# Attention and a LoRA feed-forward on one core: scores also in the projections' bank, row sums inverted on turned blocks, one sum over four key tiles, a new order in the unit

## The reference

```python
q = (hidden_states @ Wq).reshape(b, s, 32, 32)
kv = hidden_states @ Wkv;  k, v = kv[..., :32], kv[..., 32:]
scores = einsum('bqhd,bkd->bhqk', q, k) * 32 ** -0.5
scores = where(causal, scores + slopes * (key_pos - query_pos), -inf)
out = einsum('bhqk,bkd->bqhd', softmax(scores), v).reshape(b, s, h) @ Wo
x = layernorm(x + out)
x = layernorm(x + x @ W.T + b + lora_of_the_chosen_rank(x))
```

## Time and profile before

| what | value |
|---|---|
| median of 3 runs | 3776.58 us (3774.8 to 3776.71) |
| the profiled execution | 3775.03 us |
| its span in the trace | 3773.2 us |
| attention, first to last score tile | 68.4 to 2863.5 us |
| TensorE busy by the records | 3582.0 us (95%) |
| VectorE, ScalarE, GpSimd busy | 2415.6, 1927.6, 1358.9 us |
| mean granted TensorE clock | 0.984 |

### The profile page before, as it was taken

The page is one execution under the profiler, slowest core; times in us unless marked ns, Lnnn a source line. Parts: engine busy times, 40 slices in busy tenths (PEclk is TensorE's granted clock), DMA queues, the critical chain, the costliest instruction groups (busy, mean ns, idle before and its releaser), DMA issues. The chain is left out here.

```text
span 3773.2 us, 56666 instructions
## 1 busy us (share of the span) xinstructions
PE 3582.0 (95%) x21057; PEld 2207.2 (58%) x21057; DVE 2415.6 (64%) x5438; ACT 1927.6 (51%) x3252; POOL 1358.9 (36%) x419
## 2 busy tenths in 40 slices
PE   5899999999999999899999999999995999999998
PEld 4555554455444444555554455544432888989987
DVE  4777777777776763777777777777742444444444
ACT  2656656666676756656666666676764101001000
POOL 1114444544455544124445554454552011011010
PEclk8999999999999999999999999999997999999999
DMA  2121110010000011111110000000003121121221
GB/s 85 46 60 32 49 32 24 24 38 23 21 15 21 15 35 32 49 57 32 49 32 24 24 15 23 21 15 21 10 7 123 45 67 55 62 67 50 67 67 40
DMA packets 157358, 148.11 MB, mean 39 GB/s; under 512 B 8356, under 2 KB 140452, under 8 KB 155016
## 3 DMA queue, kind: packets, MB, share of 16 engines
q1 hardware_dynamic: 157128, 145.07, 13.1%
HBM read 94.13 MB, written 33.62 MB: 34 GB/s over the span
## 5 line engine op out<-in xcount | busy, mean ns | idle before, releaser
L507 ACT ACTIVATE prob<-ps_s,alibi 128x512 f32<-128x512 f32 (+3 forms) x2560 | 1525.5, 623 | 868.6 <-PE ps_s L777 435.7
L452 POOL TENSOR_TENSOR prob<-prob 128x2048 f32<-128x2048 f32 (+1 forms) x240 | 1046.8, 4362 | 1091.4 <-ACT prob L507 1091.4
L587 DVE TENSOR_REDUCE mxp<-ps_a 128x1 f32<-128x512 f32 x1536 | 984.1, 682 | 384.4 <-PE ps_a L707 376.1
L774 PE MATMUL ps_s<-qst,kexp 97*128 97x512 f32 (+3 forms) x2560 | 1047.9, 417 | 42.5 <-ACT prob L507 28.4
L707 PE MATMUL ps_a<-kmax,qst 97*128 97x512 f32 (+3 forms) x2560 | 961.9, 396 | 38.8 <-DVE mxp L590 23.1
L774 PEld LDWEIGHTS ps_s<-qst,kexp 97*128 97x128 f32 x2560 | 481.6, 189 | 788.5 <-ACT prob L507 613.5
L719 PE MATMUL ps_o<-prob,val 128*32 128x512 f32 (+3 forms) x5120 | 602.1, 542 | 6.0 <-ACT prob L507 6.0
L590 DVE CUSTOM_DVE_ANT_0 ps_a<-ps_a,maska 128x128 f32<-128x128 f32 (+3 forms) x1024 | 495.4, 503 | 163.0 <-PE ps_a L707 130.1
L707 PEld LDWEIGHTS ps_a<-kmax,qst 97*128 97x128 f32 x2560 | 489.3, 194 | 113.4 <-DVE mxp L590 47.2
L972 POOL TENSOR_TENSOR hb_sb<-h_sb,bias_b 128x1024 f32<-128x1024 f32 x32 | 76.8, 2401 | 792.7 <-DVE z_sb L1116 732.4
L719 PE MATMUL ps_sum<-prob,ones 128*32 128x512 f32 (+3 forms) x3200 | 347.0, 513 | 0.0
(11 more groups left out here) (147 smaller groups left out, 3673.7 us busy)
## 6 DMA issues: line engine op xcount, KB each, us to landing
wq_raw<-in_L_attn_Wq SPq DMA_DIRECT2D x64, 512.0 KB, 3.9
xs<-in_L_attn_hidden_states SPq DMA_DIRECT2D x8, 2048.0 KB, 8.1
qst<-qst SPq DMA_DIRECT2D x64, 256.0 KB
att_scratch<-at_sb SPq DMA_DIRECT2D x64, 256.0 KB, 2.4
at_raw<-att_scratch SPq DMA_DIRECT2D x32, 512.0 KB, 5.2
x_sb<-in_L_attn_hidden_states SPq DMA_DIRECT2D x32, 512.0 KB, 4.2
out<-z_sb SPq DMA_DIRECT2D x32, 512.0 KB, 3.1
z_sb<-in_L_attn_Wo SPq DMA_DIRECT2D x4, 512.0 KB, 5.4
```

The costliest lines, as they stand in the source:

```text
L452: nc.gpsimd.tensor_tensor(even[:, :, c1:], even[:, :, c1:], odd[:, :, c1:], ALU.add).then_inc(pair_done, 1)
L507: nc.scalar.activation(prob[slot_of(steps + k)][:, h, c0:], ps_s[h % 2][:, c0:], ACT.Exp, bias=alibi_of(g, h, k - full_tiles(g))).then_inc ...
L587: nc.vector.tensor_reduce(top, ps, AX.X, ALU.max).then_inc(a_done, 1)
L774: last = nc.tensor.matmul(bank[:, c0:], kexp[0:KR, at:at + P], qst[g % 3][0:KR, h, c0:], start=True, stop=not diagonal)
```

## The change

- Score tiles may use `ps_m` as a third bank, from a slot that `third_from` gives (the last QE or VT, plus THIRD) to the end of the unit; `score_places` takes, for each tile, the bank whose last use is longest ago, and TensorE waits for that use's exponential. The next unit's first projection waits for the last exponential out of `ps_m`.
- In units of 16 key tiles, GpSimd adds two pairs to a quad (ADDQ) and one product sums the four tiles (SQ).
- The row sums are equal on the 32 partitions of a head. VectorE now turns `ps_sum` in 32x32 blocks, takes reciprocals of one column of each block, and turns them back with a broadcast. The copy into `s_sb` is gone.
- `PROBS` is 8, and the tables of slots have other numbers.

```diff
-PROBS = 6
+PROBS = 8
+def adds_until(g, k):
+    pair = k // 2
+    quad = pair // 2
+    if quad < quads_summed(g):
+        return adds_before(g) + 3 * quad + 1 + pair % 2
+    return adds_before(g) + quads_summed(g) + pair + 1
-CHUNKS_AHEAD = (8, 13, 23, 27)
-A_END = (9, 17, 25, 33)
-A_FROM = (11, 18, 26, 34)
-Q_AT = ((0, 0.5), (0, 1), (0, 1.25), (1, 1.5))
-QE_AT = ((3, 1), (7, 2), (9, 3), (11, 5))
-CT_AT = (11, 18, 30, 38)
-X_AT = ((7, 0.5), (9, 1.25), (19, 2), (22, 3))
-KV_AT = (11, 25, 35, 46)
-VT_AT = (17, 27, 40, 47)
-PV_AT = (1, 1, 1, 1)
-SM_AT = (1, 1, 3, 3)
-WS_AT = (5, 17, 27, 33)
-RECIP_AT = ((0, 2, 3, 8, 11), (6, 16, 25, 29, 30), (22, 27, 44, 45, 46), (20, 36, 60, 61, 62))
+CHUNKS_AHEAD = (7, 14, 18, 19)
+A_END = (8, 17, 31, 41)
+A_FROM = (13, 18, 31, 41)
+Q_AT = ((0, 0.5), (0, 1), (1, 1.25), (0, 1.75))
+QE_AT = ((3, 1), (7, 2), (9, 3), (12, 4))
+CT_AT = (12, 22, 35, 42)
+X_AT = ((4, 0.25), (8, 1.75), (19, 1.5), (19, 3.25))
+THIRD = (6, 6, 2, 4)
+QUADS = (0, 0, 0, 1)
+QUAD_AT = 7
+KV_AT = (10, 23, 33, 41)
+VT_AT = (17, 28, 47, 49)
+PV_AT = (1, 1, 2, 1)
+SM_AT = (2, 1, 2, 1)
+WS_AT = (5, 21, 31, 28)
+RECIP_AT = ((0, 2, 3, 4, 11), (0, 2, 3, 5, 14), (0, 2, 5, 7, 18), (0, 2, 4, 5, 20))
+def third_from(g):
+    if g + 2 >= UNITS:
+        return 0
+    s = seg_of(g) % NSEG
+    return (VT_AT[s] if prepares(g) else QE_AT[s][0] + (GH - 1) * QE_AT[s][1]) + THIRD[s]
+def score_places():
+    last = [None, None, None]
+    places = []
+    for g in range(UNITS):
+        if g + 2 < UNITS:
+            last[2] = None
+        for slot in range(GH * ktiles(g)):
+            free = range(3 if slot >= third_from(g) else 2)
+            bank = min(free, key=lambda b: -1 if last[b] is None else last[b])
+            places.append((bank, last[bank]))
+            last[bank] = len(places) - 1
+    return places
...
+            if k >= QUAD_AT and (k - QUAD_AT) % 4 == 0 and (k - QUAD_AT) // 4 < quads and h == SM_AT[s]:
+                out.append(("SQ", (k - QUAD_AT) // 4))
+        if k % 4 == 3 and k // 4 < quads:
+            out.append(("ADDQ", k // 4))
...
                     if what == "OE":
-                        act.wait_ge(sm_done, START + steps + ktiles(g))
+                        act.wait_ge(pv_done, START + steps + ktiles(g))
                         act.wait_ge(at_done, START + g)
                         nc.scalar.activation(o_sb[:], ps_o[:], ACT.Copy).then_inc(o_copied, 1)
-                        nc.scalar.activation(s_sb[:], ps_sum[:], ACT.Copy).then_inc(o_copied, 1)
...
-                nc.vector.reciprocal(r_sb[:, cols], s_sb[:, cols]).then_inc(r_done, 1)
+                if part == 0:
+                    dve.wait_ge(sm_done, START + steps_before(g + 1))
+                    nc.vector.transpose(sum_t[:].rearrange("p b d -> p (b d)"), ps_sum[:]).then_inc(sum_turned, 1)
+                elif part == 1:
+                    dve.wait_ge(sum_turned, START + g + 1)
+                    nc.vector.reciprocal(inv_t[:], sum_t[:, :, 0]).then_inc(inv_done, 1)
+                elif part == 2:
+                    dve.wait_ge(inv_done, START + g + 1)
+                    dve.wait_ge(at_done, START + g)
+                    nc.vector.transpose(r_sb[:].rearrange("p (b d) -> p b d", d=DH),
+                                        inv_t[:].unsqueeze(2).broadcast_to([P, QB // DH, DH])).then_inc(r_done, 1)
...
                     if what == "S":
-                        pe.wait_ge(e_done, START + max(0, GH * (steps + k) + h - 1))
+                        if before is not None:
+                            pe.wait_ge(e_done, START + before + 1)
+                        elif place == 2 and prepares(g):
+                            pe.wait_ge(vt_done, START + seg_of(g) + 2)
+                        elif place == 2:
+                            pe.wait_ge(ql_done, START + GH * min(UNITS, g + 3))
...
                     if what == "PV":
-                        if arg == ktiles(g) - 1:
-                            pe.wait_ge(e_done, START + GH * (steps + arg + 1))
+                        pe.wait_ge(e_done, START + GH * (steps + arg + 1))
```

More of the change, by code:

```diff
@@ L72, in pairs_summed, with quads_summed, adds_in, adds_before @@
     return ktiles(g) // 2 - 1 if full_tiles(g) else 0
-def pairs_before(g):
-    return sum(pairs_summed(x) for x in range(g))
+def quads_summed(g):
+    return QUADS[seg_of(g) % NSEG]
+def adds_in(g):
+    return pairs_summed(g) + quads_summed(g)
+def adds_before(g):
+    return sum(adds_in(x) for x in range(g))
+def adds_until(g, k):
[4 more added lines that the diff above has]
+    return adds_before(g) + quads_summed(g) + pair + 1
 def ring(sg):
@@ L166, in plan_unit @@
     recip_at = {x: part for part, x in enumerate(RECIP_AT[s])}
-    summed = pairs_summed(g)
+    summed, quads = pairs_summed(g), quads_summed(g)
     for k in range(n):
@@ L265, in attention @@
         ps_m = pb(ctx, "ps_m", [P, QB])
+        ps_s.append(ps_m)
+        places = score_places()
         counters = []
@@ L300, in attention @@
         o_copied = counter("o_copied")
+        sum_turned = counter("sum_turned")
+        inv_done = counter("inv_done")
         r_done = counter("r_done")
@@ L429, in divide @@
             def divide(g):
-                pool.wait_ge(r_done, START + QT * (g + 1))
+                pool.wait_ge(r_done, START + g + 1)
+                pool.wait_ge(o_copied, START + g + 1)
                 pool.wait_ge(at_out, START + 16 * g)
@@ L453, in step @@
                                                 ALU.add).then_inc(pair_done, 1)
+                    if what == "ADDQ":
+                        one, two = (prob[slot_of(steps + 4 * arg + i)] for i in (0, 2))
+                        pool.wait_ge(pair_done, START + adds_until(g, 4 * arg + 3))
+                        nc.gpsimd.tensor_tensor(one[:], one[:], two[:], ALU.add).then_inc(pair_done, 1)
             units(prologue, step, lambda count: divide(UNITS - 1))
@@ L739, in prologue, with in_third @@
                 turn_max(0, FIRST - 1)
+            def in_third(g):
+                return max([i + 1 for i in range(tiles_before(g)) if places[i][0] == 2], default=0)
             def step(g, plan, count):
@@ L753, in step @@
                     if what == "Q":
+                        if arg == 0 and in_third(g):
+                            pe.wait_ge(e_done, START + in_third(g))
                         if arg == 0 and prepares(g - 1):
@@ L767, in step @@
                         c0 = max(0, k - full_tiles(g)) * P
-                        bank = ps_s[h % 2]
+                        place, before = places[GH * (steps + k) + h]
+                        bank = ps_s[place]
                         if arg == (0, 0):
                             pe.wait_ge(c_in, START + 16 * (g + 1))
-                        pe.wait_ge(e_done, START + max(0, GH * (steps + k) + h - 1))
+                        if before is not None:
[4 more added lines that the diff above has]
+                            pe.wait_ge(ql_done, START + GH * min(UNITS, g + 3))
                         diagonal = k >= full_tiles(g)
@@ L779, in step @@
                     if what == "PV":
-                        if arg == ktiles(g) - 1:
-                            pe.wait_ge(e_done, START + GH * (steps + arg + 1))
+                        pe.wait_ge(e_done, START + GH * (steps + arg + 1))
                         if arg == 0:
-                            pe.wait_ge(o_copied, START + 2 * g)
+                            pe.wait_ge(o_copied, START + g)
                         over_keys(g, ps_o, val[:, key_tile(g, arg)], arg).then_inc(pv_done, 1)
+                    if what in ("SM", "SP", "SQ") and arg == 0:
+                        pe.wait_ge(sum_turned, START + g)
                     if what == "SM":
+                        pe.wait_ge(e_done, START + GH * (steps + arg + 1))
                         over_keys(g, ps_sum, ones[:], arg).then_inc(sm_done, 1)
                     if what == "SP":
-                        pe.wait_ge(pair_done, START + pairs_before(g) + arg + 1)
+                        pe.wait_ge(pair_done, START + adds_until(g, 2 * arg + 1))
                         over_keys(g, ps_sum, ones[:], 2 * arg).then_inc(sm_done, 2)
+                    if what == "SQ":
+                        pe.wait_ge(pair_done, START + adds_until(g, 4 * arg + 3) + 1)
+                        over_keys(g, ps_sum, ones[:], 4 * arg).then_inc(sm_done, 4)
             units(prologue, step, lambda count: None)
```

10 lines of the change are left out of this document (4 added, 6 removed).

## The result

| kernel | median, us | lowest to highest | ratio to before, 95% interval |
|---|---|---|---|
| before | 3776.64 | 3774.8 to 3778.94 | |
| changed | 3690.52 | 3688.47 to 3707.25 | 0.9783 [0.9768, 0.9797] |

A forecast was written before the change was run, and what follows sets the result against it. TensorE's own order of work was taken as the frame, with 231 us of waits inside it. Terms 48 + 13 + 14 + 9 + 14.5 + 3 = 101.5 us off 3776.6 gave 3675; range for 8 in 10: 3615 to 3725.

The forecast's parts named there:

- third bank: Scores also in `ps_m` late in units: ScalarE has three tiles queued across a product, fewer TensorE waits, 48 us.
- quad: Units of 16: GpSimd adds replace one row-sum product of 1.19 us on TensorE; 13 us, bounds 3 and 19.
- inversion, units of 4 key tiles: Row sums inverted on turned blocks shorten VectorE's chain in units of 4 key tiles: 16 x 0.9 = 14 us.
- VT later than KV: Unit 29: eight slots between KV and VT remove a 6.2 us wait and the lower clock behind it; 9 us.
- other units at ends of segments: Units 13, 15, 21, 23 and twins lose waits at VT or reciprocals on VectorE; 14.5 us, bounds 0 and 25.
- end of attention: From the last reciprocal to the division's end, a ScalarE copy and 3.39 us become shorter; 3 us, bounds 0 and 3.4.
- met before: TensorE's added waits for exponentials ahead of products: already met by the preceding score tile's wait, except with three banks; costed at nothing.
- Rival 3: Units of 16: GpSimd late with the four-tile sum, products wait, 48 us go; 3723 us, chance 0.09.
- taking 0.94 out of that chain brings the whole unit forward by it: Units of 4 key tiles: VectorE's last reciprocal in slot 8 goes, so each unit ends 0.9 us earlier.
- rival 1: Whole order fits better: waits ahead of the bank's opening halve, all behind it go; 155 us, 3621, chance 0.13.
- Rival 2: Waits move to ScalarE, whose exponentials become the pace; only 51 us faster, 3725, chance 0.11.
- Rival 4: More short waits between matmul groups lower the clock in 48 units, 4.3 us each; slower, 3880, chance 0.05.

The follow-up runs named there:

- the second experiment: Changed kernel with SM_AT back from 2 to 1 and CT_AT from 12 to 11 in units of 4 key tiles: 3690.49 us, ratio 0.9771.
- The first experiment: Changed kernel with row-sum products moved away from the products with the values (SM_AT 3) in units of 12 and 16: 3718.77 us, ratio 0.9846.

## Why the prediction was nearly right

| term | forecast, us | measured, us |
|---|---|---|
| third bank | 48 | 37 alone; 111 in the new order |
| quad | 13 | 13.7 (13.0 in the units of 16) |
| inversion, units of 4 key tiles | 14 | plain units 0.2 longer; alone 0.1 shorter, 5 in the whole kernel |
| VT later than KV | 9 | alone: unit 29 8.5, whole kernel 7.2 |
| other units at ends of segments | 14.5 | 1.4 longer (13, 15, 21, 23 and twins) |
| end of attention | 3 | 2.8 |
| row sums joined to the other product | 0 | 28 |

**Third bank.** The step from waits to gain held in kind, with less in size. Alone the bank took 0.5 off a plain unit of 8, 0.4 off one of 12 and 1.3 off one of 16 (32.9, 48.8 and 62.5 us), where the sum had 0.45, 0.8 and 1.7. In units of 12 slot 20 begins 0.57 us late, since the bank's first tile waits for the last copy of q, for which the prediction had taken off 0.3. Units 62 and 63 gained 3.5 and 1.7 alone, not 4 each; the latter has 6.8 us at half the clock. What failed is that the bank was costed on the order of before: the new order asks more of it, and without it would have lost 25 us. The added waits ahead of the products, which the prediction put at nothing as "met before", are often not met (387 weight loads wait), but cost TensorE nothing that shows.

**Quad.** The size is right, partly by luck. The prediction took one lone product of 1.19 away and lost a third of it to waits. The product that went was one of a joined pair, worth 2.04 - 1.19 = 0.85, and a plain unit gained more than that, 1.05, since slot 33 is 0.2 shorter as well (2.23 for 2.43). Units 62 and 63 gave 0.1 and -2.1. The quad's own product is in time in plain units; the later one of slot 41 is not quite, at no cost. Rival 3 came true in unit 63, where no chunks stand between the score tiles.

**Inversion.** The durations were right. The step that failed is "taking 0.94 out of that chain brings the whole unit forward by it". VectorE's chain did get shorter, but the next wait stood 0.3 us behind: a score tile that waits for its bank. In the alone version this is shown. In the changed kernel more is against it. The last chunks are reached 0.3 to 0.6 us later, with the two of one slot together. With the old row sums and CT, in the second experiment's timeline, TensorE waits there:

```profile
144.11 0.51 PE L774 MATMUL ps_a<-kmax,qst 97*128 97x512 f32 x1 [0.70 <-DVE mxp L647]
```

Slot 5 takes 3.62 us there, 2.60 before. That the order of the chunks is what takes the gain was only argued. The third bank with the old table of chunks and the turned inversion would test it; it was not tried. The other units of 4 (5 to 7 and 37 to 39) are 7.4 us shorter in the changed kernel, but not all by the inversion: 7 and 39 lose 2.3 and 2.5 with it alone, while 5 and 37 (1.3 each) lose a wait of 1.39 us at VT, which the new places of X, KV and VT take away. And alone, in the new slots of R, the inversion costs 0.3 us in each plain unit of 8 and 12, which the sum did not have.

**VT.** Right in place, size and clock: of the six waits of the earlier trace rows only the one of 3.2 us ahead of unit 0 is left, and the clock in unit 29 is 1.00. Attention has six stretches at a clock of 0.5 before (37.5 us together) and seven after (30.7 us); the one of 13.7 us behind the wait of the earlier trace rows and those of units 5 and 37 are gone, those in units 17, 45, 48 and 63 are new.

**Other units.** Mis-sized by 16 us. Fewer reciprocals on VectorE bought nothing there: 21 and 53 got 1.1 longer each. In unit 13 the wait at VT was only 0.50 us; slot 26 begins 0.8 us earlier, but the unit ends only 0.2 earlier; half of what is lost is in its last slot, 1.94 us (1.66). All units of 8 have that: the new table puts a chunk into the last slot, which is why plain ones take 33.2 and not 32.9. Unit 45 got 1.4 longer by the clock: it has a stretch of 3.4 us at 0.5 from slot 28, which 13 has not. Units 15 and 47 differ by 4 us in both kernels in the same way (10.2 us at 0.5 in 15 alone). The first experiment takes 64.1 and 62.5 in 21 and 53, so joining is not what made them longer; what did was not settled.

**End of attention**, in the timeline after, against the earlier trace rows:

```profile
2784.15 0.72 DVE L669 STREAM_TRANSPOSE sum_t<-ps_sum 128x512 f32<-128x512 f32 x1 [50.59 <-PE ps_sum L786]
2784.90 0.25 DVE L672 RECIPROCAL inv_t<-sum_t 128x16 f32<-128x16 f32 x1
2785.19 0.71 DVE L676 STREAM_TRANSPOSE r_sb<-inv_t 128x512 f32<-128x512 f32 x1
2785.98 1.26 POOL L487 TENSOR_TENSOR at_sb<-o_sb,r_sb 128x512 f32<-128x512 f32 x1 [4.47 <-DVE r_sb L676]
```

From the first operation of the inversion to the division's end it is 3.09 us, and ScalarE's copy lies beside it. From the end of the last row-sum product to the division's end it is 3.15 us, against 5.91 before: 2.8 us won.

**What was not in the sum.** `PV_AT` and `SM_AT` were read as numbers of slots and costed at nothing, though they put two products side by side. This is the largest omission, 28 us of gain. It offset what the inversion and the other units did not bring, so that the total is nearer than its terms is luck. Two numbers beside the sum are off: the 70 us of waits that bound the bank's term add up to 64 by the counts given, and the 3200 and 3072 records are the row-sum products of all units, not of those of 16.

**The rivals.** Plain units of 12 and 16 did better than forecast, as rival 1 has it, but by joined products rather than by its mechanism: ahead of slot 28 unit 27 gained 1.4 us (slot 28 begins 27.7 us into the unit, 29.1 before), and without the quad, which took the row sums out of slots 19 and 27, nothing (29.3). Rival 2 appears in the second line of the waits but did not cancel the gain. Rival 4 did not decide the changed kernel: its plain units in the windows above show a clock of 1.00 with three banks in rotation, against the Trainium skill's case ("TensorE: Matmul & The Clock Gate", A second HAM failure mode). Of the other plain units one, 17, has a stretch at 0.5 (49.0 us for 47.3). But the rival's mechanism is real here: the old order with bank and joined products has 24 stretches, ten of them behind a wait of 1.4 to 1.6 us for the third bank in units of 12. Its price was too high, 4.3 us a drop from unit 29, where a stretch of 3.4 us costs 1.4.

## What to carry to other kernels

A buffer and the order that uses it have to be costed together. Five of the kernels read: 3777 (old order), 3741 (with the bank), 3797 (bank and joined products), 3801 (new order without the bank), 3691 (new order with it).

Where one engine's chain ends a unit, find the wait that stands next behind it before counting the relief: 0.76 us won on VectorE came out as 0.1, since a score bank was 0.3 us away.

A table of slots is also a table of neighbours. When two entries fall on the same slot, cost the pair from a row that shows it, and ask how long the other engines are left without work.

## What the runs showed of the hardware

Two products over 128x512, each in four groups of 32 columns, cost 2.04 us of TensorE side by side and 2 x 1.19 apart between score tiles: keeping them together saves 0.34 us a pair. A 32x32-block transpose of 128x512 fp32 on VectorE took 0.716 us out of PSUM and 0.705 with a source that is one column broadcast: about the time of a plain pass over the tile (0.682). Some waits of TensorE cost more than their length, since a stretch at the granted clock of 0.5 (1.2 GHz, the lower of its two levels) followed: 13.7 us of it, beginning inside a wait of 6.2 us, in unit 29 before, 3.4 us behind 2.60 in unit 63, where a product of 1.04 took 1.83, and 3.4 to 6.8 us behind 1.59 in eight of ten plain units of 12 with bank and joined products. Each 3.4 us there cost 1.4. Waits of 0.50 in the same place, with the bank alone, were followed by none.
